# Attention: later keys of the exact scores masked by a TensorE matmul instead of zeroed exponentials on GpSimd

## The reference, cut to what matters

```python
scores = jnp.einsum('bthd,bshd->bhts', q, k)
mask = jnp.tril(jnp.ones((T, T), dtype=scores.dtype))
scores = scores * mask
attn = jax.nn.softmax(scores / T ** 0.5, axis=-1)
out = jnp.einsum('bhts,bshd->bthd', attn, v).reshape(B, T, H * Dh)
```

## Time and profile before

| | us |
|---|---|
| median of 3 runs (2175.28 to 2182.58) | 2179.13 |
| the profiled execution | 2178.26 |
| its span, first to last instruction | 2176.5 |
| PE busy / PEld busy | 1987.0 / 1261.1 |
| DVE / ACT / POOL busy | 1238.4 / 818.4 / 888.6 |
| attention, from the first exact scores to the last values | about 343 to 692 of the span |
| mean granted TensorE clock | 0.946 |

### The profile page before, as it was taken

How to read it: one execution, slowest core, us unless ns; L and a number is a source line. 1 busy time by engine, 2 the same in 40 slices (tenths; PEclk the granted TensorE clock), 3 DMA queues, 4 the chain that set the end, 5 groups by cost and what they waited for, 6 DMA issues and landing times. The chain is left out here.

```text
span 2176.5 us, 29726 instructions
## 1 busy us (share of the span) xinstructions
PE 1987.0 (91%) x8876; PEld 1261.1 (58%) x8876; DVE 1238.4 (57%) x2704; ACT 818.4 (38%) x1549; POOL 888.6 (41%) x708
## 2 busy tenths in 40 slices
PE   5899958999998799968599999999999999999987
PEld 5676635556555667646455555555565555555556
DVE  6322264666775722237466666666656666667526
ACT  2122243555655122214234344444514444443423
POOL 0344410342222044422036555566415555565632
PEclk9999968999999599989579999999999999999999
DMA  9112241111110811132331221122122222221101
GB/s 392 50 61 66 54 128 29 41 33 44 31 30 8 352 59 64 63 107 112 70 73 42 53 58 46 43 58 58 34 55 59 59 54 58 58 47 42 32 0 52
DMA packets 64617, 150.91 MB, mean 69 GB/s; under 512 B 14320, under 2 KB 19648, under 8 KB 62208
## 3 DMA queue, kind: packets, MB, share of 16 engines
q1 hardware_dynamic: 54240, 120.44, 19.4%
q0 software_dynamic: 9120, 24.92, 3.7%
q10 hardware_dynamic: 1152, 4.19, 0.5%
HBM read 68.95 MB, written 18.61 MB: 40 GB/s over the span
## 5 line engine op out<-in xcount | busy, mean ns | idle before, releaser
L1858 POOL TENSOR_TENSOR mla_PS<-mla_PS,mla_PT 128x1024 f32<-128x1024 f32 x192 | 457.9, 2385 | 197.7 <-ACT mla_PT L2144 196.3
L2144 ACT ACTIVATE mla_PT<-PS 128x512 f32<-128x512 f32 x512 | 293.3, 598 | 418.8 <-PE PS L1959 373.1
L2287 DVE TENSOR_REDUCE mla_MXP<-PS 128x1 f32<-128x512 f32 x512 | 334.5, 687 | 197.6 <-PE PS L1939 195.4
L1968 PE MATMUL PS<-mla_PT,mla_CN 128*64 128x512 f32 x1024 | 274.2, 614 | 0.0
L1283 DVE TENSOR_REDUCE att_MX<-PS 128x1 f32<-128x512 f32 (+3 forms) x304 | 194.3, 660 | 86.2 <-PE PS L994 47.5
L522 DVE COPY moe_HT<-PS 128x256 f32<-128x256 f32 x188 | 70.6, 418 | 301.3 <-PE PS L648 301.3
L1939 PE MATMUL PS<-mla_KH,mla_QH 113*128 113x512 f32 x512 | 199.1, 456 | 16.2 <-DMA mla_KL<-mla_SL 16.1
L1959 PE MATMUL PS<-mla_QH,mla_KH 113*128 113x512 f32 x512 | 210.3, 411 | 1.7 <-ACT mla_QH L2128 1.5
L684 POOL DMA_INDIRECT moe_XS<-rows_in,moe_GI x96 | 93.6, 975 | 266.7 <-PE PS L634 131.2
L1959 PE MATMUL PS<-mla_QL,mla_KH 113*128 113x512 f32 x512 | 201.9, 394 | 0.0
L1959 PE MATMUL PS<-mla_QH,mla_KL 113*128 113x512 f32 x512 | 201.6, 394 | 0.0
(11 more groups left out here) (295 smaller groups left out, 3100.4 us busy)
## 6 DMA issues: line engine op xcount, KB each, us to landing
W<-in_W_dram SPq DMA_DIRECT2D x16, 2048.0 KB, 28.3
mla_QH<-mla_SH SPq DMA_DIRECT2D x64, 128.0 KB, 2.4
mla_KH<-mla_SH SPq DMA_DIRECT2D x64, 128.0 KB, 2.4
mla_QL<-mla_SL SPq DMA_DIRECT2D x64, 128.0 KB, 2.5
mla_KL<-mla_SL SPq DMA_DIRECT2D x64, 128.0 KB, 2.4
mla_KH<-mla_SH SPq DMA_DIRECT2D x64, 96.0 KB, 2.4
mla_KL<-mla_SL SPq DMA_DIRECT2D x64, 96.0 KB, 2.4
sums_Y<-rows_out SPq DMA_DIRECT2D x9, 512.0 KB, 6.3
```

The source lines that it names most:

```text
L1858: pool.tensor_tensor(PS[:, :], PT[:, slot(0), :] if k == 1 else PS[:, :], PT[:, slot(k), :], ALU.add).then_inc(s_ps.handle, 1)
L1968: ins = pe.matmul(bank(6)[h * DKVL:(h + 1) * DKVL, :], CN[:, b, k, 0:DKVL], PT[:, slot(k), h * HB:(h + 1) * HB], start=(k == 0), stop=(k = ...
L2144: act.activation(PT[:, slot(k), h * HB:(h + 1) * HB], bank(st_bank(s, h))[:, :], ACT.Exp, scale=MLA_SCALE).then_inc(s_p.handle, 1)
L2287: dve.tensor_reduce(MXP[:, n // NPC, c, h, t:t + 1], bank(piece_bank(n))[:, :], AX_X, ALU.max).then_inc(s_mx.handle, 1)
```

## The change

- `cut_later_keys`, its semaphore and its 16 calls per group are gone from GpSimd; `clear_max_rows` no longer waits for it.
- In the slots whose key tile lies on the diagonal, PE adds to the first 128 score columns of each of the two heads a matmul of the stationary IDR with a new constant PASTQ, -1e30 where the key is later than the query. The exponentials there come out as zero.
- `values_of` waits for the exponentials in every slot.
- VectorE makes PASTQ from SLOW at the start, behind a wait for SLOW; the first rough scores wait for one more count of the constants' semaphore.

```diff
-                def cut_later_keys(G, s):
-                    q, j = key_of(s // 2)
-                    if j < 4 * q:
-                        return
-                    c0 = columns(q, j)
-                    part = PT[:, s // 2 % 2, 2 * (s % 2):2 * (s % 2) + 2, c0:c0 + P]
-                    pool.wait_ge(s_p.handle, s_p.at(NSL * G + s + 1))
-                    pool.affine_select(part, part, [[0, 2], [1, P]], ALU.is_ge, 0.0, base=0, channel_multiplier=-1).then_inc(s_cut.handle, 1)
...
-                        pool.wait_ge(s_cut.handle, s_cut.at(NCUT * (H - 2) + cuts(18)))
...
-                        cut_later_keys(G, s)
...
-                            pe.wait_ge(s_c.handle, s_c.at(3))
+                            pe.wait_ge(s_c.handle, s_c.at(4))
...
                     for hh in range(2):
                         ins = pe.matmul(st_banks(s)[:, hh, c0:HB], KT[:, G % 2, pair, j * P:(j + 1) * P], QT[:, G % 2, 2 * pair + hh, q * HB + c0:(q + 1) * HB],
-                                        start=True, stop=True)
+                                        start=True, stop=j < 4 * q)
+                    if j >= 4 * q:
+                        for hh in range(2):
+                            ins = pe.matmul(st_banks(s)[:, hh, c0:c0 + P], IDR[:, :], PASTQ[:, :], start=False, stop=True)
                     ins.then_inc(s_st.handle, 1)
 
                 def values_of(G, kk):
                     q, j = key_of(kk)
-                    if j >= 4 * q:
-                        pe.wait_ge(s_cut.handle, s_cut.at(NCUT * G + cuts(2 * kk + 2)))
-                    else:
-                        pe.wait_ge(s_p.handle, s_p.at(NSL * G + 2 * kk + 2))
+                    pe.wait_ge(s_p.handle, s_p.at(NSL * G + 2 * kk + 2))
...
+                dve.wait_ge(s_c.handle, s_c.at(3))
+                dve.tensor_scalar(PASTQ[:, :], SLOW[:, :], -UNSEEN, None, ALU.mult).then_inc(s_c.handle, 1)
```

More of the change, by code:

```diff
@@ L79 @@
     "att_low_parts", "att_rows_placed", "att_first_half_placed", "att_rough_scores", "att_piece_max", "att_block_max", "att_maxT_in_psum", "att_max_rows", "att_later_weight",
-    "att_scores", "att_probs", "att_later_keys_cut", "att_values_added", "att_outT_copied", "att_out_in_psum", "att_later_part", "att_out_sum",
+    "att_scores", "att_probs", "att_values_added", "att_outT_copied", "att_out_in_psum", "att_later_part", "att_out_sum",
     "att_out_denominator", "att_out_rows", "att_outrowsT_in_psum", "att_outrowsT_copied", "att_projected", "att_x_updated", "lora_weights",
@@ L714, in attention_stage @@
     s_sh, s_mx, s_mb, s_mt, s_nm, s_e0 = S("rough_scores"), S("piece_max"), S("block_max"), S("maxT_in_psum"), S("max_rows"), S("later_weight")
-    s_st, s_p, s_cut, s_v = S("scores"), S("probs"), S("later_keys_cut"), S("values_added")
+    s_st, s_p, s_v = S("scores"), S("probs"), S("values_added")
     s_oc, s_bt, s_f1, s_f2, s_rc, s_ao = S("outT_copied"), S("out_in_psum"), S("later_part"), S("out_sum"), S("out_denominator"), S("out_rows")
@@ L763, in columns @@
         return P * max(0, j - 4 * q)
-    NCUT = 2 * TB
-    def cuts(slots):
-        return max(0, slots - TB)
     FILL = (3, 6, 10, 16, 18, 21)
@@ L795, in attention_stage @@
         MX, MB, E0 = sb("MX", [P, 2, 2, HG, 4]), sb("MB", [P, P + 4]), sb("E0", [P, 2, HG, 4])
-        IDR, LATER = sb("IDR", [P, P], F32R), sb("LATER", [P, P], F32R)
+        IDR, LATER, PASTQ = sb("IDR", [P, P], F32R), sb("LATER", [P, P], F32R), sb("PASTQ", [P, P], F32R)
         expert = g.sums.buffers(ctx, PT[:, :, :, :].rearrange("p u h (n d) -> p (u h n) d", d=D))
```

## The result

The changed kernel takes 2185.87 us in the median of 20 runs, against 2179.38 for the kernel before in as many: a ratio of 1.0028, 95% interval 1.0019 to 1.0036, or 6.5 us more. 2189 had been forecast, slower, within 2179 to 2200.

A forecast was written before the change was run, and what follows sets the result against it. PE was taken to bound the stage, with VectorE next. Masking pairs add 15.7 us and two removed waits take away 5.6, so +10.1 on 2179.13 gives 2189 us, range 2179 to 2200.

The forecast's parts named there:

- about half of the pairs hidden: Masking pairs on PE, slots 8 to 23: 30.1 us if nothing were hidden, 15.7 us added after hiding behind waits.
- two late places in GpSimd's queue: Ends of groups 2 and 7, where PE waits for late zeroing: removing these waits takes away 5.6 us.
- The price of a pair: Two 128-column masking matmuls on PE, each with its own weight load: 0.235 us a pair.
- Rival 1: Weight loads of a pair hide behind matmuls, 0.12 us a pair; time stays at 2179.5 us; chance 0.22.
- Rivals 2 and 3: 2: VectorE's pace swallows everything, 2173.5 us, chance 0.06. 3: nothing is hidden, +24.5, 2203.6 us, chance 0.14.
- Slots 13 and 14: Group 5: two pairs, 0.47 us, less the 0.28 us wait at 604.91; 0.19 us passes.
- Slots 15 and 16: Group 5: of the 0.32 us wait at 608.99, 0.23 us taken as hidden; 0.24 us passes.
- The wait at 608.99: Group 5, PE's loads wait 0.32 us, partly under a streaming matmul; 0.23 us taken as hiding added work.
- Group 2: Zeroings queue behind later_tiles additions; PE idles 2.78 us, then clock falls to 0.52; gain 4.5 us, between 3.6 and 5.4.
- The end of group 7: Last zeroing stands behind out_rows in GpSimd's queue and the last values idle for it; gain 1.1 us.
- Group 7: No rough pieces, so no waits for reductions; all slots but 9 and 10 pass their pairs, 3.3 us.
- Nothing elsewhere: Outside the two late places PE waits for GpSimd only tenths, so removing the zeroing there is worth nothing.

The follow-up runs named there:

- the second dose: The changed kernel with each masking matmul issued twice: 2204.48 us, ratio 1.0122 to the kernel before.
- the two small experiments: The kernel before, zeroing kept, with masking matmuls only in slots 9 and 10 (2179.67 us, one run) or only in 11 and 12 (2190.7 us, one run, not read).

## Why the prediction was right

Sign, mechanism and range were right: about half of the pairs hidden, two late places in GpSimd's queue given back. Of the added time, 15.7 us were forecast and 13.1 measured; of the gain, 5.6 and 7.2. Both errors point the same way, so that +10.1 became +6.5. The windows, which repeat better than whole runs, give 12.9 and 6.3: the changed kernel less the one without masks is 10.45 us longer in groups 0 to 6 and 2.44 from there to the last update of x.

Step by step for group 5, where what a slot passes is the distance of a slot's start to the next, changed kernel less kernel before:

| slots | forecast to pass, us | measured, us |
|---|---|---|
| 8 | 0.24 | 0.19 |
| 9, 10 | 0 | 0.00 |
| 11, 12 | 0.47 | 0.43 |
| 13, 14 | 0.19 | 0.08 |
| 15, 16 | 0.24 | 0.10 |
| 17, 18 | 0.17 | 0.22 |
| 19, 20 | 0.47 | 0.42 |
| 21 to 23, and 0 of group 6 | 0 | 0.02 |
| sum | 1.78 | 1.46 |

Slot 16 needs its own rows, first before (PE, then the load of its second rough piece), then in the changed kernel:

```profile
608.43 0.69 PE L1014 MATMUL PS<-att_QT,att_KT 128*128 128x512 f32 x2
609.00 0.44 PE L991 MATMUL PS<-att_KT,att_QT 128*128 128x384 f32 x1
...
609.46 0.44 PE L991 MATMUL PS<-att_KT,att_QT 128*128 128x384 f32 x1
609.46 0.19 PEld L991 LDWEIGHTS PS<-att_KT,att_QT 128*128 128x128 f32 x1 [0.17 <-DVE att_MX L1283]
```

```profile
614.88 0.67 PE L998 MATMUL PS<-att_QT,att_KT 128*128 128x512 f32 x2
...
615.57 0.39 PE L975 MATMUL PS<-att_KT,att_QT 128*128 128x384 f32 x1
...
615.85 0.39 PE L975 MATMUL PS<-att_KT,att_QT 128*128 128x384 f32 x1
```

- **The price of a pair** was 0.235; the slots of group 5 that pass one show 0.19 to 0.23. Rival 1, 0.12 a pair, is out by the second dose (0.23). The Trainium skill's 81 ns for each of a stream of such matmuls (TensorE: Matmul & The Clock Gate, Back-to-back issue gap) is lower than what the trace shows, 0.11 to 0.115; here the measurement decides.
- **Hidden, or passing.** Rivals 2 and 3 are out by the two small experiments: in groups 1 and 3 to 5 pairs in slots 9 and 10 cost nothing, in 11 and 12 everything. The steps that were mis-sized are "Slots 13 and 14" and "Slots 15 and 16": together the four slots pass 0.18, not 0.43. In slot 16 a second wait, at 609.46, had no term, and it hid the most. The wait at 608.99, of which I took 0.23, hid only 0.1: the first rough piece comes 0.69 us after the scores, where it came after 0.57. The second piece follows it after 0.28 us, where it took 0.46. Slots 13 and 14 hide 0.36 by the pair's 0.22, more than the 0.28 for which the load at 604.91 waited.
- **Group 2.** I took 4.5 between 3.6 and 5.4; without masks it gains 5.1. The end of group 7 was put at 1.1 and is 1.4 without masks.
- **Group 7** was to pay 3.3 for its pairs. It pays 2.0 up to its last scores and 2.4 up to the last update of x (changed kernel less the one without masks); the more that the run with masks and zeroing shows goes with the low clock of its tail. With 1.4 gained the net is 1.1, where 2.2 had been forecast. I had let all its slots but 9 and 10 pass in full. Against the kernel before, slots 13, 18 and 21 pass 0.08, 0.00 and 0.03, five others 0.16 to 0.18, and slot 9 passes 0.17.
- **Nothing elsewhere** holds: without the zeroing groups 1, 4, 5 and 6 do not move by more than 0.02 us. PASTQ is made within VectorE's wait at the start, as forecast: 2.69 us of that wait are left behind it.
- **The range of the forecast itself**, 2184 to 2196, was added up a little too high: a third or two thirds hidden, less 4.7 or 6.5 gained, make 2182.7 to 2194.5.

Not settled: the 2 us by which the first exact scores come later in the changed kernel's profile. They are ahead of any mask, and the start of that stretch moves as much among the other kernels (342.4 to 346.6 with the new constant, 342.8 and 344.4 without it); it was not tried apart.

## What to carry to other kernels

Before work is moved off a busy engine, look at who waits for it: here 51.9 us of GpSimd were worth 6 to 7, nearly all of it at two places where something else stood ahead of it in the queue, and putting that queue in another order got 5 of these for nothing. In this kernel the bound engine's waits hid added work where the wait belonged to a run of the other engine that had already begun; where the other engine idled for this one, the addition passed in full or nearly so, and that can be read slot by slot from the two timelines. In groups 1 to 6 a masking matmul of 64 columns cost as much as one of 128.

## What was not expected

In group 2 PE's pause for GpSimd of 2.78 us was followed by a granted clock of 0.52, near the lower of TensorE's two levels, 1.2 GHz; with the masks ahead of it the pause was 2.3 us, and the clock stayed at 1.00. Of the 5.1 us that group 2 gains without masks 2.8 are the pause. The other 2.3 are the work behind it, which took 5.49 us at 0.52 (485.69 to 491.18) and takes 3.19 us at 1.00 without masks and zeroing (483.42 to 486.61).

The run with masks in slots 11 and 12 has the same work at a clock between: 4.63 us at 0.64 (488.54 to 493.17). Its pause ahead of that work was 2.77 us, as long as before, so the clock differed behind pauses of one length, and whether the shorter pause is what kept it up beside all masks is not shown.
